# Layer 0's experts with the tokens stationary, loads ordered by first use, four PSUM banks for layer 1's first batch, and new orders for layer 0's turns

## Chip, core, metric

One core of one Trainium2 chip. The metric is the device time of one execution in microseconds; three runs of the kernel before gave 2697.05, 2699.24 and 2699.74 us, median 2699.24.

## What is computed

Four layers on an input `x` of 16 batches x 256 tokens x 128 features. Each layer normalises `x` and adds an attention (or state space) part and a feed-forward part:

```python
x  = L0_attn_x
xn = layernorm(x)
x  = x + L0_attn(xn) + L0_ffn(xn)   # 16-head attention, then a Mamba block; 32 experts
xn = layernorm(x)
x  = x + L1_attn(xn) + L1_ffn(xn)   # 16 heads of 64; feed-forward in FP4 blocks of 16
...                                 # layers 2 and 3: not touched by the change

# L0_ffn: every expert picks 8 tokens of each batch, and works on their weighted sum
merged = einsum('bked,bke->bed', tok, vals)        # [16 batches, 32 experts, 128]
h = gelu(einsum('bei,eih->beh', [merged, 1], w1))  # w1 [32, 129, 512]
o = einsum('bej,ejo->beo', [h, 1], w2)             # w2 [32, 513, 128]
out = scatter_add(o * vals)                        # back to the tokens picked
```

## The kernel before, in words

Five queues (TensorE `pe`, VectorE `ve`, ScalarE `ac`, GpSimd `po`, and `sp`, which issues nearly all DMAs) run lists of instructions that wait on each other's semaphores. A stage is a Python generator; its pieces are laid out between `yield`s, and `merge` interleaves the stages that run side by side by the places given in the table `ORDER` (lines 228 to 302), a list of numbers for each engine and stage. So the order of the work within a turn is written out by hand, per engine, and every turn of a layer has the same order.

**Load** (`load`, L2353). SP issues `x` (2 MB in rows of 512 bytes), then the packs `wf`, `wf0`, `wb` (masks and identity) and `wfc` (convolution weights). All engines wait for all packs, VectorE for `x` also. VectorE casts the masks to bf16 (L2363), TensorE multiplies two weights into `w_step` (L2367), ScalarE takes an exponential, VectorE builds `w_tap` (L2378). SP stores zeros twice. Then all five engines meet at a barrier (`phase_end`).

**Layer 0** (`layer0`, L2404). `pre` of a batch (L330, L1064, L1681) normalises it, turns it, computes the gate of the experts and `q`, `k`, `v`, all through one PSUM bank, so that its steps alternate between TensorE and the engine that empties the bank. For its idle filler `pe_idle` (L324) TensorE multiplies the mask by the identity with no use of the result. `pre` of batch 0 runs alone, `pre` of batch 1 beside the first row maxima (`FIRST[0]`). Then 19 turns follow. Turn t has `pre` of batch t+2, `wide` (scores, maxima, exponentials, values) of t, `out` and `inner` of t-1 (attention output; Mamba projections, `delta`), `states` of t-2 (eight pieces of the scan, each with two reads of 512 KB from DRAM that SP issues, a product and a scan on VectorE, a product on GpSimd and a sum over the states on TensorE, L868), and `results` of t-3. Turns 0 to 2 lack the later stages, turns 16 to 18 the earlier ones.

**Layer 0's experts** (`experts0`, L2430), after a barrier. For each of 32 experts: TensorE holds 128x128 blocks of `w1` stationary and moves 128 columns (16 tokens of 8 experts, of which one expert's 16 are used), 4 matmuls (L911); VectorE adds the bias (L1527); ScalarE applies GELU (L1990); TensorE does the same with `w2` (L924), 4 matmuls; VectorE adds the bias (L1532). All are fp32. Beside it VectorE quantises layer 1's feed-forward weights in three pieces (`ve_fp4` L1544, three operations per expert from expert 12 on) and TensorE turns them in nine (L973), VectorE copies them (L1604). Weights come in DMAs of 256 KB into 8 + 8 buffers; the first 8 experts are loaded behind the last reads of layer 0 (L2425), then `wf1` (3.2 MB), then the other 24.

**Layer 1** (`layer1`, L2449) begins after another barrier with `pe_spread1` of batches 0 and 1 and then `pre1` of batch 0 alone: 8 steps of two 256-column matmuls (L404), each emptied by ScalarE (L1719), and 4 steps of one 512-column matmul (L409), each emptied by VectorE (L1128), all through bank 4, each waiting until the bank has been read.

## Time and profile before

| | us |
|---|---|
| three runs, median | 2699.24 |
| profiled execution, its own time | 2694.34 |
| its span, first to last instruction | 2692.9 |
| load, to the barrier | 24.0 |
| layer 0 before its experts | 24.0 to 909.9 |
| layer 0's experts | 910.0 to 971.4 |
| layer 1 begins | 971.5 |

The page's busy shares of the span are TensorE 81%, VectorE 73%, ScalarE 53%, GpSimd 29%. A share is an average over stages with different limits, so the prediction reads stretches of the span instead. "PEclk" is the clock that TensorE was granted: 1.00 is 2.4 GHz, 0.50 is 1.2 GHz, and what lies between is a mix of the two over the stretch. One fp32 matmul of the program is two records in the trace (x8 is four matmuls).

### The profile page before, as it was taken

How to read it: one execution, taken by the hardware profiler on the slowest of the kernel's cores; microseconds unless marked ns; L12 is line 12 of the kernel's file. 1: busy time of each engine (PE TensorE's matmuls, PEld its weight loads, DVE VectorE, ACT ScalarE, POOL GpSimd, SP SyncE). 2: the span in 40 equal slices, each digit the busy share in tenths (PEclk: the TensorE clock that was granted, in tenths of full speed). 3: DMA queues.
4: the chain of work that ended last, by engine and by line, in shares of the span. 5: the costliest groups of instructions: out<-in, count | busy, mean ns of one | idle time of the engine just before them, and what ended most of it. 6: DMA issues, size and time to landing. Idle time of an engine off the chain costs nothing.

```text
span 2692.9 us, 47200 instructions
## 1 busy us (share of the span) xinstructions
PE 2176.3 (81%) x18050; PEld 1497.0 (56%) x18205; DVE 1959.5 (73%) x3999; ACT 1428.7 (53%) x3672; POOL 775.5 (29%) x460
## 2 busy tenths in 40 slices
PE   4678877887875678999999999868888986887886
PEld 2445555554542555666666666645565655555553
DVE  3389999899888537777777777745666642799997
ACT  1355565555554216767767676613343432566664
POOL 0034444443445302333323333310000000344443
PEclk9899899898987778999999999979999998778876
DMA  2077777786788940000000000000100000788886
GB/s 84 14 181 183 189 178 191 173 198 168 175 215 214 283 140 1 1 1 1 1 1 1 1 1 1 1 27 22 30 23 16 6 22 22 181 197 195 198 194 155
DMA packets 114320, 261.84 MB, mean 97 GB/s; under 512 B 13552, under 2 KB 55280, under 8 KB 113584
## 3 DMA queue, kind: packets, MB, share of 16 engines
q1 hardware_dynamic: 112048, 254.63, 37.6%
...
## 4 chain that ended last, share of the span: by engine, by line
PE 50%; DVE 20%; ACT 12%; DMA 8%; issue 8%; SPq 2%; another core or an unknown queue 0%; POOL 0%; POOLq 0%; DVEq 0%; ACTq 0%
DMA h<-dtu_rows 6%; PE psum L327 3%; DVE h L1481 3%; PE psum L695 3%; PE psum L691 3%; ACT pr L1840 3%; PE psum L582 3%; PE psum L743 3%; PE psum L404 2%; PE psum L627 2%; PE psum L702 2%; PE psum L431 2%; DVE mx L1396 2%; ACT pt L1884 2%; PE psum L700 2%
## 5 line engine op out<-in xcount | busy, mean ns | idle before, releaser
L2083 POOL TENSOR_TENSOR h<-h,Crep 128x1024 f32<-128x1024 f32 x128 | 322.4, 2520 | 563.9 <-DVE h L1481 563.9
L2067 POOL TENSOR_TENSOR pr<-pr,rsum 128x512 f32<-128x512 f32 x192 | 236.0, 1236 | 548.2 <-DVE rsum L1362 548.2
L1481 DVE TENSOR_TENSOR_SCAN h<-dA,h 128x1024 f32<-128x1024 f32 x128 | 305.2, 2387 | 18.8 <-ACT dA L1980 18.8
L1396 DVE TENSOR_REDUCE mx<-psum 128x4 f32<-128x1024 f32 (+1 forms) x192 | 230.2, 1216 | 106.0 <-PE psum L700 106.0
L1884 ACT ACTIVATE pt<-psum 128x1024 f32<-128x1024 f32 x192 | 189.1, 1020 | 142.1 <-PE psum L702 142.0
L1980 ACT ACTIVATE dA<-dA,A 128x255 f32<-128x255 f32 x512 | 215.6, 499 | 74.0 <-DMA dA<-delta_rows 73.6
L1840 ACT ACTIVATE pr<-psum,nb 128x256 f32<-128x256 f32 (+1 forms) x512 | 210.5, 429 | 15.9 <-DVE nb L1354 14.9
L2118 POOL TENSOR_TENSOR h<-h,Crep 128x1024 f32<-128x1024 f32 x64 | 151.3, 2364 | 223.2 <-DVE h L1289 223.2
L1850 ACT ACTIVATE prT<-psum 128x512 f32<-128x512 f32 x192 | 116.0, 604 | 149.7 <-PE psum L596 147.7
L1474 DVE TENSOR_TENSOR h<-h,psum 128x1024 f32<-128x1024 f32 x128 | 153.0, 1207 | 39.3 <-DMA h<-dtu_rows 39.1
L404 PE MATMUL psum<-xnT,pack_wf 128*128 128x256 f32 x512 | 148.4, 414 | 25.9 <-ACT qT L1719 18.6
L695 PE MATMUL psum<-qT,kT 32*128 32x256 f32 (+1 forms) x2048 | 123.2, 371 | 55.3 <-DVE mx L1396 54.8
L1350 DVE TENSOR_REDUCE mx<-psum 128x2 f32<-128x512 f32 (+1 forms) x192 | 130.5, 679 | 27.0 <-PE psum L586 16.4
L1289 DVE TENSOR_TENSOR_SCAN h<-dA,h 128x1024 f32<-128x1024 f32 x64 | 148.5, 2320 | 0.1
L327 PE MATMUL psum<-mask,identb 128*128 128x512 bf16 x433 | 123.5, 417 | 28.5 <-DVE qT L1089 20.0
...
L695 PEld LDWEIGHTS psum<-qT,kT 32*128 32x128 f32 x2048 | 86.9, 206 | 89.0 <-DVE mx L1396 69.9
L691 PE MATMUL psum<-kT,qT 32*128 32x128 f32 (+1 forms) x2048 | 115.4, 352 | 25.5 <-ACT pt L1884 13.2
L582 PE MATMUL psum<-kT,qT 64*128 64x256 f32 (+1 forms) x1024 | 112.4, 350 | 27.0 <-ACT pr L1840 27.0
L404 PEld LDWEIGHTS psum<-xnT,pack_wf 128*128 128x128 f32 x512 | 93.6, 198 | 63.6 <-ACT qT L1719 27.6
L743 PE MATMUL psum<-pt,v 128*32 128x256 f32 (+1 forms) x2048 | 96.5, 329 | 30.5 <-ACT pt L1884 29.9
L1792 ACT ACTIVATE dA<-dA,A 128x255 f32<-128x255 f32 x256 | 108.3, 495 | 21.8 <-DMA dA<-delta_rows 21.7
...
## 6 DMA issues: line engine op xcount, KB each, us to landing
dA<-delta_rows SPq DMA_DIRECT2D x192, 512.0 KB
h<-dtu_rows SPq DMA_DIRECT2D x192, 512.0 KB, 6.5
...
pack_wf<-wf SPq DMA_DIRECT2D x1, 3192.0 KB, 11.8
...
```

What stands on the lines that cost most here:

```text
L327: k.pe.e.matmul(bk[:, :], k.w["identb"], k.w["mask"], start=True, stop=True, skip_group_check=True)
L404: i = pe.e.matmul(B4[:, (g - g0) * L:(g - g0 + 1) * L], w[f"w{n}1"][:, g, :], xnT[:, :], start=True, stop=True)
L582: pe.e.matmul(k.bank[r][:, n * wid:(n + 1) * wid], qT[rows, g, q * P:(q + 1) * P], kT[rows, g, 0:wid], start=n == 0, stop=True, skip_group ...
L691: pe.e.matmul(banks[r][:, cols], qT[row:row + 32, g, q0:q0 + P], kT[row:row + 32, kg, 0:wid], start=n == 0, stop=True, skip_group_check=True)
L695: pe.e.matmul(banks[r][:, cols], kT[row:row + 32, kg, k0:k0 + P], qT[row:row + 32, g, k0:L], start=n == 0, stop=True, skip_group_check=True)
L1396: ve.e.tensor_reduce(mx[:, qb, 2 * h:2 * h + 2, groups[0]:groups[-1] + 1], k.psum[:, base:base + 2, :].rearrange("p i (n x) -> p i n x", n ...
L1481: ve.e.tensor_tensor_scan(flat(h), flat(k.dA[n % NDA]), flat(h), 0.0, ALU.mult, ALU.add).then_inc(*k.set("scanned", 0, n))
L1840: i = ac.e.activation(pr[:, h * wid:(h + 1) * wid], bk[:, h * wid:(h + 1) * wid], ACT.Exp, bias=nb[:, h:h + 1], scale=float(HD[1]) ** -0.5 ...
L1884: ac.e.activation(k.pt[2 * c + h][:, :], k.psum[:, base:base + 2, :].rearrange("p i x -> p (i x)"), ACT.Exp, scale=float(HD[l]) ** -0.5).t ...
L1980: i = ac.e.activation(dA[:, s, 1:], dA[:, s, 1:], ACT.Exp, scale=k.A0[:, n % 8, s:s + 1])
L2067: po.e.tensor_tensor(p3, p3, bcast(k.rsum[n][:, 0:len(heads[r])], P * (q + 1), 2), ALU.mult).then_inc(*k.set("normed", 1, b, p, r))
L2083: po.e.tensor_tensor(h[:, :, :], h[:, :, :], bcast(k.Crep[b % 2][:, :], 4, 1), ALU.mult).then_inc(*k.set("hC", 0, n))
```

## The change

1. **Load.** The first four tiles of `x`, `wf` and `wf0` go first and are all that TensorE, VectorE and ScalarE wait for. `pre` of batch 0 runs next. Casts, `w_step`, `A` and `w_tap` follow in `prepare_*`, behind it. The rest of `x` is loaded last. The barrier goes. The two filler matmuls of `pre` of batch 0 go.
2. **Turns.** `ORDER[0]` is replaced (small swaps), and turns 0, 1, 2, 15, 16, 17 and 18 have orders of their own.
3. **Experts.** Four experts a group. 32 columns of `merged` are stationary for each expert in a column tile of its own, and `w1` is moving, 512 columns. ScalarE copies the result, TensorE turns it with four transposes, VectorE adds the bias, ScalarE applies GELU; the output matmuls hold the tokens in column tiles and move `w2`; ScalarE copies, TensorE transposes, VectorE adds. Weights come as 16 DMAs of 1 MB (two experts, 8 KB a partition), ten buffers, seven of them loaded behind the last reads. A quantisation runs in one go at groups 2, 3 and 5; the turns at groups 4, 6 and 8.
4. **Layer 1's first batch** goes through banks 5, 7, 2, 4 in rotation.

```diff
+def places(layer, turn):
+    return ORDER.get(f"{layer}.{turn}", ORDER[layer])
...
 ORDER = {
     0: {
-        "pe_pre0": (2, 8, 9, 13, 20, 21, 26, 34),
+        "pe_pre0": (5, 10, 11, 14, 21, 23, 30, 34),
-        "ve_out": (7, 8, 10, 16, 18, 22),
+        "ve_out": (2, 4, 8, 10, 15, 22),
-        "ve_states": (2, 4, 19, 21, 23, 25, 31, 34, 36, 37, 41, 43, 44, 45, 49, 50, 52),
+        "ve_states": (1, 3, 20, 23, 24, 25, 31, 34, 36, 37, 42, 43, 44, 45, 49, 50, 52),
...
+    '0.0': {
+        "pe_pre0": (4, 5, 6, 8, 11, 13, 14, 15),
+        "pe_wide0": (0, 1, 2, 3, 7, 9, 10, 12, 16, 17),
...
-LOADS = {"x": 0, "wf": 1, "wb": 2, "wf0": 3, "wfc": 0, "wf0e": 0, "wf1": 1, "wf2": 2, "wf3": 3}
+LOADS = {"x0": 0, "wf": 1, "wb": 2, "wf0": 3, "wfc": 4, "x": 5, "wf0e": 0, "wf1": 1, "wf2": 2, "wf3": 3}
...
-    pe_idle(k, bk, 2)
+    if b:
+        pe_idle(k, bk, 2)
...
+FIRST_BANKS = (5, 7, 2, 4)
+def bank_of1(k, b, n):
+    return k.bank[4 if b else FIRST_BANKS[n % 4]]
+def taken1(k, b, n):
+    if b == 0:
+        if n < 4:
+            return k.at("xnT", 1, 0)
+        n -= 3
+    return evacuated(k, 1, b, n - 1) if 0 < n <= len(QK[1]) else k.at("v", 1, b, n - 9) if n else k.at("xnT", 1, b)
...
-QUANT_AT = (12, 17, 22)
-TURN_AT = (18, 19, 20, 23, 24, 25, 28, 29, 30)
+EG = P // 32
+NG0 = E0 // EG
+NPAIR, NEARLY = 10, 7
+QUANT_AT = (2, 3, 5)
+TURN_AT = ((), (), (), (), (0, 1, 2), (), (3, 4, 5), (), (6, 7, 8), (), ())
 def pe_experts0(k):
+    for g in range(NG0 + 3):
+        x = g - 2
+        if 0 <= x < NG0:
+            pe.wait_ge(*k.at("hg", x))
+            if x:
+                pe.wait_ge(*k.at("o0", x - 1))
             for j in range(J):
+                for c in range(EG):
+                    i = pe.e.matmul(k.bank[4][32 * c:32 * c + 32, 0:P], flat(k.hg[x % 2][:, j, c:c + 2, :]), expert_w2(k, EG * x + c, j),
+                                    start=j == 0, stop=j == J - 1, tile_position=(0, 32 * c), skip_group_check=True)
+        x = g - 3
+            pe.e.transpose(k.bank[5][:, 0:P], k.o0[x % 2][:, :], w["ident"]).then_inc(*k.set("o0_turned", x))
+        x = g - 1
+            z = k.z[x % 2][:, :].rearrange("t (p j) -> t p j", j=J)
             for j in range(J):
+                i = pe.e.transpose(k.bank[2 + x % 2][:, j * P:(j + 1) * P], z[:, :, j], w["ident"])
+        if g < NG0:
+            for c in range(EG):
+                i = pe.e.matmul(k.bank[g % 2][32 * c:32 * c + 32, :], flat(k.merged[:, ex:ex + 2, :]), expert_w1(k, ex),
+                                start=True, stop=True, tile_position=(0, 32 * c), skip_group_check=True)
+        for i in TURN_AT[g]:
+            pe_weight1(k, i)
...
 def ac_experts0(k):
+        if g < NG0:
+            ac.e.activation(k.z[g % 2][:, :], k.bank[g % 2][:, :], ACT.Copy).then_inc(*k.set("z", g))
+        if g in QUANT_AT:
+            ac_weights1(k, QUANT_AT.index(g))
+        x = g - 1
+            ac.e.activation(k.hg[x % 2][:, :, 0:EG, :], k.hz[x % 2][:, :, :, :], ACT.Gelu).then_inc(*k.set("hg", x))
+        x = g - 2
+            ac.e.activation(k.o0[x % 2][:, :], k.bank[4][:, 0:P], ACT.Copy).then_inc(*k.set("o0", x))
...
 def sp_experts0(k, some):
+    for n in some:
+        if n >= NPAIR:
+            sp.wait_ge(*k.at("output0", (n - NPAIR) // 2))
+        sp.e.dma_start(flat(k.pairs[n % NPAIR]), k.ins["m_w"][n, :, :]).then_inc(*k.set(f"pair{n % NPAIR}", n, by=16))
...
 def load(k, packs):
+    sp.e.dma_start(k.X[:, 0:2 * QT, :], x[:, 0:2 * QT, :]).then_inc(*k.set(*landed("x0"), by=16))
+    for pname in ("wf", "wf0", "wb", "wfc"):
+        sp_load(k, pname, packs[pname])
+    sp.e.dma_start(k.X[:, 2 * QT:, :], x[:, 2 * QT:, :]).then_inc(*k.set(*landed("x"), by=16))
...
+    for q in (pe, ve, ac):
+        for pname in ("x0", "wf", "wf0"):
+            q.wait_ge(*k.at(*landed(pname)))
...
+def prepare_ve(k):
+    ve.wait_ge(*k.at(*landed("wb")))
+    for n, t in k.small:
+        ve.e.tensor_copy(t[:, :], w[n])
+    ve.wait_ge(*k.at("dt", "weights"))
+    ve.e.tensor_copy(flat(k.w_step), k.bank[0][:, :])
+    ve.wait_ge(*k.at("A_exp", 0))
+    ve.e.tensor_scalar(k.A[:, :, :], k.A[:, :, :], -1.0, None, ALU.mult)
+    ve.wait_ge(*k.at(*landed("wfc")))
+    for j in range(CONV):
+        i = ve.e.tensor_tensor(k.w_tap[:, j, :, :], w["w_in"][:, 0:CI, :], w["conv_rows"][:, j, :, :], ALU.mult)
+    i.then_inc(*k.set("prepared"))
+    ve.wait_ge(*k.at(*landed("x")))
...
 def layer0(k, t0e):
         run(pre(k, 0))
+        prepare(k)
         merge(FIRST[0], (first(k, 0), e + "_first"), (pre(k, 1), e + "_pre0"))
...
-    sp_experts0(k, range(8))
+    sp_experts0(k, range(NEARLY))
```

## Rows read from the trace of the kernel before

**Rows 1.** The page's head.
```profile
span 2692.9 us, 47200 instructions
```

**Rows 2.** Stretches: us, busy us of each engine (instructions), clock, DMA share, GB/s.
```profile
0.00:24.00 24.00, 2.04 (x4) 1.16 (x4) 4.25 (x20) 1.51 (x2) 1.16 (x5) 1.00 0.70 235
...
64.00:108.00 44.00, 29.78 (x278) 18.43 (x280) 16.01 (x32) 10.33 (x20) 0.00 (x0) 0.79 0.01 1
108.00:155.00 47.00, 33.75 (x317) 22.83 (x319) 23.20 (x43) 20.88 (x41) 2.35 (x1) 0.95 0.41 101
...
248.00:840.00 592.00, 463.37 (x4369) 304.26 (x4412) 535.40 (x623) 340.00 (x690) 243.72 (x99) 0.91 0.77 188
840.00:880.00 40.00, 19.33 (x121) 10.32 (x120) 33.95 (x24) 19.11 (x44) 20.83 (x8) 0.67 0.90 222
880.00:910.00 30.00, 9.82 (x68) 3.55 (x66) 21.64 (x14) 5.33 (x14) 17.80 (x6) 0.59 0.84 228
...
910.00:972.00 62.00, 60.28 (x522) 58.83 (x522) 31.83 (x120) 11.13 (x37) 0.45 (x1) 1.00 0.80 257
...
976.00:1013.00 37.00, 25.68 (x46) 12.00 (x45) 3.83 (x10) 7.49 (x19) 0.00 (x0) 0.51 0.25 95
```

**Rows 3.** Timeline of batch 0's `pre`: start us, us, engine, line, [idle before].
```profile
24.01 0.49 DVE L1040 BATCH_NORM_STATS2 stats<-X 128x6 f32<-128x128 f32 x2 [2.26 <-SPq L179]
...
35.02 1.04 PE L327 MATMUL psum<-mask,identb 128*128 128x512 bf16 x2 [0.97 <-DVE qT L1089]
...
40.40 0.16 DVE L1104 TENSOR_TENSOR v<-psum,pack_wf 128x16 f32<-128x16 f32 x1
```

**Rows 4.** DMA issues (KB each, us to landing), and stretches of the load.
```profile
pack_wf<-wf SPq DMA_DIRECT2D x1, 3192.0 KB, 11.8
...
pack_wf<-wf SPq DMA_DIRECT2D x1, 1326.5 KB, 7.3
...
6.00:8.00 2.00, 0.00 (x0) 0.00 (x0) 0.00 (x0) 0.00 (x0) 0.00 (x0) 1.00 1.05 288
...
14.00:16.00 2.00, 0.00 (x0) 0.00 (x0) 0.00 (x0) 0.00 (x0) 0.00 (x0) 1.00 1.00 406
```

**Rows 5.** The chain of waits near the end of layer 0: start us, us, what.
```profile
880.77 12.06 DMA h<-dtu_rows
```

**Rows 6.** Page and timeline: what the experts' new steps are costed by.
```profile
L1850 ACT ACTIVATE prT<-psum 128x512 f32<-128x512 f32 x192 | 116.0, 604 | 149.7 <-PE psum L596 147.7
...
380.60 1.17 PE L691 MATMUL psum<-kT,qT 32*128 32x128 f32 x32
...
383.53 1.07 PE L868 MATMUL psum<-h,pack_wf 128*32 128x256 f32 x16
...
862.50 0.64 PE L868 MATMUL psum<-h,pack_wf 128*32 128x256 f32 x8 [1.30 <-POOL h L2083]
...
914.63 1.06 PE L911 MATMUL psum<-merged,w1r 128*128 128x128 f32 x8
...
932.78 0.54 DVE L1550 TENSOR_REDUCE f4s<-pack_wf 128x24 f32<-128x384 f32 x1
...
940.14 0.56 DVE L1588 SCALAR_TENSOR_TENSOR wgu_q<-pack_wf,f 128x384 uint32<-128x384 uint32 x1
```

**Rows 7.** Timeline: layer 1's first batch, and TensorE's clock coming back.
```profile
906.00 1.91 PE L327 MATMUL psum<-mask,identb 128*128 128x512 bf16 x4 [0.33 <-issue]
...
908.58 0.61 PE L890 MATMUL psum<-pack_wf,yT 128*128 128x128 f32 x4
...
978.65 2.07 PE L404 MATMUL psum<-xnT,pack_wf 128*128 128x256 f32 x4 [1.53 <-ACT xnT L1711]
980.76 0.84 ACT L1719 ACTIVATE qT<-psum,pack_wf 128x256 f32<-128x256 f32 x2 [2.16 <-PE psum L404]
...
1011.26 2.08 PE L409 MATMUL psum<-pack_wf,xnT 128*128 128x512 f32 x2 [0.78 <-DVE v L1128]
...
1024.49 1.03 PE L404 MATMUL psum<-xnT,pack_wf 128*128 128x256 f32 x4
```

More of the change, by code:

```diff
@@ L401, in pe_pre1 @@
         yield
[L402 removed]
+        pe.wait_ge(*taken1(k, b, j))
         for g in range(g0, g0 + 2):
[L404 removed]
+            i = pe.e.matmul(bank_of1(k, b, j)[:, (g - g0) * L:(g - g0 + 1) * L], w[f"w{n}1"][:, g, :], xnT[:, :], start=True, stop=True)
         i.then_inc(*k.set("qk", 1, b, j))
@@ L407, in pe_pre1 @@
         yield
-        pe.wait_ge(*(k.at("v", 1, b, j - 1) if j else evacuated(k, 1, b, 7)))
-        pe.e.matmul(B4[:, 0:cn], xnT[:, q * P:(q + 1) * P], w["wv1"][:, c0:c0 + cn], start=True, stop=True).then_inc(*k.set("v_mm", 1, b, j))
+        pe.wait_ge(*taken1(k, b, len(QK[1]) + j))
+        pe.e.matmul(bank_of1(k, b, len(QK[1]) + j)[:, 0:cn], xnT[:, q * P:(q + 1) * P], w["wv1"][:, c0:c0 + cn], start=True, stop=True).then_inc(*k.set("v_mm", 1, b, j))
 def pe_pre2(k, b):
@@ L930, in pe_ffn, with expert_w1, expert_w2 @@
+def expert_w1(k, ex):
+    return k.pairs[ex // 2 % NPAIR][:, ex % 2, 0:H0]
+def expert_w2(k, ex, j):
+    return k.pairs[ex // 2 % NPAIR][:, ex % 2, H0 + j * D:H0 + (j + 1) * D]
 def pe_ffn(k, b):
@@ L2387, in load, with prepare_ac, prepare_pe @@
     sp.wait_ge(*k.at("delta_stored1", "zero"))
-    for q in (k.pe, ve, ac, k.po, sp):
-        phase_end(k, q, "load")
+    ac.e.preload_act_table_set("natural_log_exp_and_others")
+    for x in k.x1T:
+        ve.e.memset(x[:, 0:CONV - 1], 0.0)
+    for v in k.v:
+        ve.e.memset(v[:, :, :, 9:], 0.0)
+        ve.e.memset(v[:, :, :, 8:9], 1.0)
+    for q in (pe, ve, ac):
+        for pname in ("x0", "wf", "wf0"):
+            q.wait_ge(*k.at(*landed(pname)))
+def prepare_ac(k):
+    ac = k.ac
+    ac.e.activation(k.A[:, :, :], k.w["A_log0"], ACT.Exp).then_inc(*k.set("A_exp", 0))
+    ac.wait_ge(*k.at("prepared"))
+def prepare_pe(k):
+    pe, w = k.pe, k.w
+    for m in range(CI):
+        i = pe.e.matmul(k.bank[0][:, m * DI:(m + 1) * DI], w["w_dtin"][:, m * P:(m + 1) * P], w["w_dt"], start=True, stop=True)
+    i.then_inc(*k.set("dt", "weights"))
+    pe.wait_ge(*k.at("prepared"))
+def prepare_ve(k):
+    ve, w = k.ve, k.w
+    ve.wait_ge(*k.at(*landed("wb")))
+    for n, t in k.small:
+        ve.e.tensor_copy(t[:, :], w[n])
+        w[n] = t[:, :]
+    ve.wait_ge(*k.at("dt", "weights"))
[7 more added lines that the diff above has]
+    ve.wait_ge(*k.at(*landed("x")))
 def turn0(k, t, e, pre, out, wide, inner, states, results, summing=None):
-    merge(ORDER[0],
+    merge(places(0, t),
           (results(k, t - 3), e + "_results") if results is not None and 0 <= t - 3 < NB else None,
@@ L2405, in layer0 @@
     k.slot_read, k.pre_read = [None] * 4, None
-    for e, pre, first in (("pe", pe_pre0, pe_first_max), ("ve", ve_pre0, ve_first_max)):
+    for e, pre, first, prepare in (("ve", ve_pre0, ve_first_max, prepare_ve), ("pe", pe_pre0, pe_first_max, prepare_pe)):
         run(pre(k, 0))
+        prepare(k)
         merge(FIRST[0], (first(k, 0), e + "_first"), (pre(k, 1), e + "_pre0"))
     run(ac_pre0(k, 0))
+    prepare_ac(k)
     run(ac_pre0(k, 1))
@@ L2571, in build @@
     t0e = k.pack("wf0e")
-    k.w1r = [k.sb("w1r", [P, H0]) for i in range(8)]
-    k.w2r = [k.sb("w2r", [P, H0 // P, D]) for i in range(8)]
-    k.hz, k.hg = k.two("hz", [P, H0 // P, NB]), k.two("hg", [P, H0 // P + P // NB - 1, NB])
+    k.pairs = [k.sb("pair", [P, 2, 2 * H0]) for i in range(5)]
+    assert k.top <= k.onT_end
+    k.top = end0
+    k.pairs += [k.sb("pair", [P, 2, 2 * H0]) for i in range(NEARLY - 5)]
     layer0(k, t0e)
@@ L2579, in build @@
     place_ffn(k)
+    top, k.top = k.top, k.onT_end
+    k.z, k.o0 = k.two("z", [P, H0]), k.two("o0", [P, P])
+    k.hz, k.hg = k.two("hz", [P, H0 // P, EG, NB]), k.two("hg", [P, H0 // P, EG + 1, NB])
+    k.pairs += [k.sb("pair", [P, 2, 2 * H0]) for i in range(NPAIR - NEARLY)]
+    assert k.top <= k.ffn_at
+    k.top = top
     experts0(k, t1)
@@ L2666, in _packs @@
     w1, w2 = g["L0_ffn_w1"], g["L0_ffn_w2"]
-    put("m_b1", w1[:, D, :].reshape(E0, H0 // P, P).transpose(2, 0, 1))
+    put("m_b1", w1[:, D, :].reshape(E0, P, H0 // P).transpose(1, 2, 0))
     put("m_b2", w2[:, H0, :].T)
```

370 lines of the change are left out of this document (251 added, 119 removed).

## The prediction

> **What bounds the kernel now.** The page's shares name no engine for the whole span [rows 1], so I read the stretches that the change touches [rows 2]. The load, 24 us, has no engine busy above 4.25 us; it waits for DMAs and ends in a barrier. Between 64 and 108 us TensorE is busy 29.8 of 44 us at a clock of 0.79, and VectorE 16.0: nobody is full, steps wait for one another. In 248 to 840 VectorE is busy 535.4 of 592 us, 90%. From 840 to 910 the DMA share is 0.90 and 0.84, so the reads of the scan set the pace. The experts, 910 to 972, are pure TensorE: 60.3 of 62 us, at full clock. And 976 to 1013 is TensorE again, but by turns with the engine that empties its one bank, 25.7 of 37 us busy and at 0.51 of the clock.
>
> **The load.** Before, VectorE starts batch 0 at 24.01 [rows 3]. Afterwards it needs 0.26 MB of `x` in rows of 512 bytes, 0.15 and 1.36 MB of weights in long rows. The DMAs ran at 288 GB/s while `x` was coming and at 406 over the wide packs [rows 4]: 0.9 + 0.4 + 3.3 = 4.6 us, behind some 2.5 us until the first bytes move, and about 1 us to notice; 8.2 us in all. (`wf0` alone took 7.3 us from issue to landing [rows 4].) So batch 0 begins 15.8 us earlier. Its two fillers, 1.04 us at half clock, go [rows 3]; TensorE waited for nothing else there, so 1.0 us is saved. What was prepared behind the load, 4.25 us of VectorE less 0.3 of memsets, that now lie in front [rows 2], comes back after `pre` of batch 0, where TensorE waits for it: +4.0, plus 0.2 for the handover. ScalarE's exponential and TensorE's four matmul records run beside VectorE's casts. `wb`, `wfc` and the rest of `x`, 3.1 MB, land by some 17 us and are first wanted at 24 to 29. Sum -12.6 us, between -10 (landing at 10.8) and -14.
>
> **Layer 0's first turns.** Nothing is removed; steps change places. In the order of before, the second row maximum waits behind three steps of `pre`, and the exponentials behind that; in turn 0 of the new one the scores and maxima go first. What can be won is idle time of TensorE that no other full engine forces: 14.2 us in 64 to 108 and 13.3 in 108 to 155 [rows 2]. The trace doesn't show the new order. The bounds are a loss of 4 us (a step put ahead of its input blocks its queue) and a gain of 20 (three quarters of that idle time). I take a third, -9.
>
> **The steady turns.** The new common order moves about six of VectorE's 52 places and four of TensorE's, each by one or two steps. VectorE has 56.6 us of idle time in the twelve turns of rows 2. I take -2 us, with bounds of -12 (a fifth of the idle time) and +6, half a microsecond a turn.
>
> **The last turns.** These wait for DMA. The last read of the scan took 12.06 us to land [rows 5], with 4.2 MB of experts' weights issued right behind it; now there are 7.3 MB behind it, in longer rows, which could take more of the engines' turns. Against that the new orders bring `inner` of the last batches, and so their reads, earlier. 10 to 16% of 70 us of DMA is unused [rows 2]. I take -2, from -8 to +4. The early weights are all in by the barrier: about 1 MB of reads at 250 GB/s and 7.3 MB at 406 from 881 on end at about 903.
>
> **The experts.** Before: 256 matmuls of 128 columns, in 64 fours; four take 1.06 us [rows 6] and overlap, so that the 64 need about 57 us, 0.89 each, of a stage of 61.4. After, for a group of four experts at full clock: hidden, four matmuls of 512 columns side by side in four column tiles. Four of 256 columns took 0.64 us alone and 0.535 in a row (x16 in 1.07) [rows 6], so about 0.64 + 0.43 = 1.07. Transposes of z, 0.89. Output, 16 matmuls of 128 columns, four at a time: sixteen such, tiled by rows, took 1.17 [rows 6]. Transpose of o, 0.22. Together 3.35 us against 7.1 before, 27 for eight groups against 57. The trace has no stationary load with a stride, as z's has; I take it as the plain one, and up to double (+0.8 a group, of which half counts) for the bound.
>
> TensorE is then no longer the bound. Between hidden of one group and output of the group before stand, on ScalarE in this order, the copy of z (0.60 by rows 6), GELU (256 columns, 0.4 by rows 7) and the copy of o (estimated at 0.25 from the same row). And VectorE now does each quantisation in one go: before it ran from 932.78 to 940.70 with three experts' biases between, 1.1 us, so 6.9 us by itself [rows 6]; behind it wait bias, GELU, and output. The walk, from the start of the stage: ScalarE's table load 1.3; `wf1` lands at 11.8, as before [rows 4]; quantisation 0 to 18.9; bias of group 2 and output bias, 0.7; quantisation 1 to 26.6; three turns through the one bank, 0.3 for the transpose and 0.3 for the copy and the handovers, 2.5, to 29; output, transposes 2.4 and bias 0.5, to 32; quantisation 2 (a little smaller, 6.7) to 38.7; bias and turns to 41.3; then the rest of group 7, 3.5 + 2.9 with the last turns 2.5, output 7, copy, transpose, bias, to 53. The DMA has 12.7 MB to bring, 31 us at 406 GB/s, under that cover; pairs 10 to 15 wait for outputs 0, 1 and 2, which come by 20 us.
>
> 53 us holds at full clock. TensorE is busy 27 + 3 of 53, 57%, in pieces. In 840 to 880, with 48%, the clock was 0.67, and in 64 to 108, with 68%, 0.79 [rows 2]. I take 0.75; of TensorE's work some 11 us is on the walk, so +3: 56 us against 61.4, or -5.5. Bounds: `wf1` landing at 9.5 and a full clock -11; all at half clock and slow strided loads +1. By rows a tiled set costs 0.1 us more alone than in a row. The Trainium skill, "TensorEngine Tiling (Array Packing)", section "Tiling Modes", says that changing the tiling mode drains TensorE, and this kernel changes it four times a group. By this rule each change would show; at the 0.1 us of the rows that is 3 us over 32 changes, half of them off the walk, and the trace agrees as far as it goes.
>
> **Layer 1's first batch.** Before: eight steps of 3.0 us (2.07 on TensorE at half clock, 0.84 on ScalarE, handovers) and four of 2.86 (2.08, and 0.78 of waiting for VectorE) [rows 7], 34.6 us from 978.65. With four banks TensorE doesn't wait. It would need 12 x 2.07 = 24.9 us if its clock stayed at half: -9.7. But unbroken work brought the clock back: filler matmuls from 906.0 on ran at half rate, and at 908.58 four records took 0.61 us, full rate [rows 7]. So two steps at 2.07, then six at 1.07 and four at 1.03 (the same instruction at 1024.49 took 1.03 [rows 7]); ScalarE needs 0.89 a step and VectorE under 0.78, both less. 4.1 + 6.4 + 4.1 = 14.6: -20. The Trainium skill, "TensorE: Matmul & The Clock Gate", section "What's actually happening", says that half rate is the default and that activity lifts it. The trace agrees with it in both directions here. On the other side the handful of small steps before (973 to 978) now begins behind a less busy TensorE and may run at half rate: +1. Sum -19, between -21 and -9.
>
> **Sum.** -12.6 - 9 - 2 - 2 - 5.5 - 19 = -50 us on the profiled execution's 2694.3 (span 2692.9 [rows 1]), so 2644. The median of the runs is 4.9 us above it; the forecast for the median is 2699.2 - 50 = 2649.
>
> **Rivals.** (a) *Clock.* The sparse experts stage lets TensorE fall to half rate, and it stays there: experts -1, layer 1's first batch -10. Sum -37, 2662. For it: 0.51 at 69% busy in 976 to 1013 [rows 2]. Against it: 906 to 908.6. By the skill's rule above it would come out only if TensorE paused between the steps. Chance 0.15. (b) *The orders bring more.* VectorE's idle share in the steady turns falls by a fifth and the first turns gain 15: -66, 2633. For it is the idle time, against it that the swaps are small. 0.2. (c) *The first load isn't earlier*, because the first packs share the engines with all that is issued behind them and land near 16: -43, 2656. 0.08. (d) *Slower.* The common order makes VectorE wait in each of the 12 or 13 steady turns: `out` now stands ahead of `pre` and, with it, of the whole queue; if the turned heads aren't there, products and scans are late, and the DMA slots with them. It decides from 50 / 13 = 3.8 us a turn. At 4.7 us a turn it would be 2710. VectorE's idle share of 10%, 4.7 us a turn, speaks for little cover; that the batch's heads have been turned from the turn before speaks against. 0.04. The forecast, with the bounds of its terms, has the other 0.53.
>
> **Numbers.** The likeliest case gives 2649. Its own terms spread by about 10 us; the range down to (b) and up to (a) is 2630 to 2667. About 0.2%, 5 us, can be told from no change. Faster 0.94, same 0.02, slower 0.04.
>
> **What would show it.** Right: batch 0's first VectorE row near 8 us and the first scores near 28; the experts' stage 53 to 58 us long with TensorE under 65% busy and VectorE's quantisations unbroken; in layer 1's first batch L404's successor without ScalarE's waits and at about 1.03 us from the third step; steady turns of 48 to 49 us. Wrong: the stage of the experts above 62 or under 48 us; twelve steps of 2.07; steady turns that differ by over 1 us.

## The result, and the profile after

The changed kernel took 2611.2 us (median of 4 runs, 2610.98 to 2612.55), the kernel before beside it 2698.9: a ratio of 0.9674, 95% interval 0.9661 to 0.9686, or 87.7 us less. The forecast was 2649, with a range down to 2630. The direction was right, the size was not: 50 us were expected and 88 came.

The profiled execution has a span of 2609.3 us against 2692.9 [rows 1], 83.6 less, so the account below is made of these two. First the page's head, then stretches of the kernel after (columns as in rows 2; 236 to 695 are the ten steady turns, 861 to 914 the experts, 921 to 936 layer 1's first batch):

```profile
span 2609.3 us, 46686 instructions
```

```profile
236.00:695.00 459.00, 370.69 (x3725) 247.97 (x3767) 430.94 (x542) 282.53 (x576) 190.17 (x81) 0.97 0.82 194
861.00:914.00 53.00, 30.90 (x369) 16.57 (x369) 26.87 (x74) 11.69 (x28) 0.00 (x0) 0.84 0.59 243
921.00:936.00 15.00, 14.06 (x52) 10.25 (x54) 3.39 (x7) 7.47 (x19) 0.00 (x0) 0.78 0.51 195
```

Then its timeline (start us, us, engine, line, [idle before <-releaser]) at batch 0's first row, the first scores, layer 0's last addition to `X`, the last expert's bias, and layer 1's first batch:

```profile
9.90 0.48 DVE L1248 BATCH_NORM_STATS2 stats<-X 128x6 f32<-128x128 f32 x2 [8.75 <-DMA pack_wf<-wf]
...
29.09 2.09 PE L873 MATMUL psum<-kT,qT 32*128 32x256 f32 x16 [2.21 <-DVE w_tap L2629]
...
860.94 0.42 DVE L1720 TENSOR_TENSOR X<-X,psum 128x256 f32<-128x256 f32 x1 [1.81 <-PE psum L1074]
...
913.94 0.27 DVE L1743 TENSOR_TENSOR oall<-psum,pack_wf0e 128x64 f32<-128x64 f32 x1 [0.48 <-PE psum L1106]
...
921.94 9.93 PE L586 MATMUL psum<-xnT,pack_wf 128*128 128x256 f32 x32 [1.53 <-ACT xnT L1922]
931.71 3.60 PE L591 MATMUL psum<-pack_wf,xnT 128*128 128x512 f32 x8
935.23 1.16 PE L764 MATMUL psum<-kT,qT 64*128 64x128 f32 x16
```

The steady turns are read most safely from one instruction that comes once a turn, the addition that makes `x1T`. One line of the code in a window from batch 3 to batch 13 gives eleven of them, with the first and the last start; so ten turns. The same row of the kernel before and after (line, engine, operation, count: shortest/median/longest in ns, first and last start us):

```profile
L1441 DVE SCALAR_TENSOR_TENSOR x1T<-psum,pack_wf,xnT x11: 466/466/476, 256.5 to 746.0; 128x256 f32<-128x256 f32 x11
```

```profile
L1649 DVE SCALAR_TENSOR_TENSOR x1T<-psum,pack_wf,xnT x11: 452/454/484, 236.0 to 694.8; 128x256 f32<-128x256 f32 x11
```

To the hundredth the starts are 256.53 and 745.98 before, 235.95 and 694.82 after: ten turns took 489.4 us and take 458.9, **48.9 us a turn before, 45.9 after**. Put together by stages:

| stage | forecast | measured |
| --- | --- | --- |
| to the first scores (40.6 to 29.1) | -12.6 | -11.5 |
| on to `x1T` of batch 3 | -9 | -9.1 |
| ten steady turns (batch 3 to 13) | -2 (for twelve) | -30.6 |
| rest of layer 0 | -2 | +2.7 |
| end of layer 0 to layer 1's first such matmul | -5.5 | -8.2 |
| layer 1's first batch (34.6 to 13.3) | -19 (with +1 of the row above) | -21.3 |
| everything behind it | 0 | -5.6 |

Of the last row, 2.0 us lie between the end of layer 1's first batch and the first gather of layer 3 (1257.4 us before, 1255.4 after), and 3.6 in the stretch from layer 3's first to its last gather (336.1 and 332.5). Layer 3's code is the same. That stretch took between 332.5 and 336.3 us in the profiles of this study, whether a kernel had this change or not, and the changed kernel profiled once more (e15) took 336.2 there; so these 3.6 us are spread between executions.

So one term failed, the steady turns.

### The profile page after: what moved, and what is told of

The parts are those of the page before. It is cut to its first block, busy times and chain, and to the rows that moved or that the text cites. A ratio compares the mean times of both kernels' runs of the same rounds, so it can differ in the third digit from the quotient of the medians.

```text
span 2609.3 us, 46686 instructions
## 1 busy us (share of the span) xinstructions
PE 2125.4 (81%) x17896; PEld 1447.2 (55%) x18051; DVE 1927.3 (74%) x3952; ACT 1427.9 (55%) x3664; POOL 771.3 (30%) x460
## 4 chain that ended last, share of the span: by engine, by line
PE 45%; DVE 21%; ACT 12%; DMA 8%; issue 7%; SPq 2%; another core or an unknown queue 0%; POOL 0%; POOLq 0%; DVEq 0%; ACTq 0%
DMA h<-dtu_rows 7%; DVE h L1689 4%; PE psum L492 3%; PE psum L877 3%; ACT pr L2052 3%; PE psum L764 3%; PE psum L873 3%; PE psum L925 2%; PE psum L809 2%; PE psum L586 2%; PE psum L613 2%; PE psum L884 2%; DVE mx L1558 2%; PE psum L748 1%; PE psum L882 1%
## 5 line engine op out<-in xcount | busy, mean ns | idle before, releaser
L1689 DVE TENSOR_TENSOR_SCAN h<-dA,h 128x1024 f32<-128x1024 f32 x128 | 297.2, 2327 | 5.8 <-ACT dA L2192 5.8
L586 PE MATMUL psum<-xnT,pack_wf 128*128 128x256 f32 x512 | 141.6, 402 | 19.9 <-ACT qT L1930 14.9
L877 PE MATMUL psum<-qT,kT 32*128 32x256 f32 (+1 forms) x2048 | 116.0, 353 | 39.9 <-DVE mx L1604 39.4
L1497 DVE TENSOR_TENSOR_SCAN h<-dA,h 128x1024 f32<-128x1024 f32 x64 | 148.3, 2318 | 0.1
L492 PE MATMUL psum<-mask,identb 128*128 128x512 bf16 x432 | 114.6, 394 | 18.9 <-ACT qT L1903 7.4
L586 PEld LDWEIGHTS psum<-xnT,pack_wf 128*128 128x128 f32 x512 | 92.1, 194 | 52.8 <-ACT qT L1930 20.9
```

Of the source, the lines that this page charges most:

```text
L492: k.pe.e.matmul(bk[:, :], k.w["identb"], k.w["mask"], start=True, stop=True, skip_group_check=True)
L586: i = pe.e.matmul(bank_of1(k, b, j)[:, (g - g0) * L:(g - g0 + 1) * L], w[f"w{n}1"][:, g, :], xnT[:, :], start=True, stop=True)
L877: pe.e.matmul(banks[r][:, cols], kT[row:row + 32, kg, k0:k0 + P], qT[row:row + 32, g, k0:L], start=n == 0, stop=True, skip_group_check=True)
L1689: ve.e.tensor_tensor_scan(flat(h), flat(k.dA[n % NDA]), flat(h), 0.0, ALU.mult, ALU.add).then_inc(*k.set("scanned", 0, n))
```

## Experiments

### Is it the common order? (e1, e2)

e1 is the kernel before with one thing changed, the dictionary `ORDER[0]`; e2 is the changed kernel with the old `ORDER[0]`:

```diff
 # e1, in the kernel before (e2: the reverse, in the kernel after)
 ORDER = {
     0: {
-        "pe_inner": (11, 18, 19, 23, 32),
+        "pe_inner": (9, 19, 20, 24, 27),
...
```

> The kernel before with the new common order of layer 0's turns in the place of the old one, for all turns; nothing else of the change. Theory A (the common order alone makes the steady turns shorter): the ten turns from x1T of batch 3 to that of batch 13 take 459 us (45.9 a turn) in place of 489.4, and the whole about 2665 (2655 to 2672). Rival B (the steady turns are shorter because the special first turns leave the batches in another phase, or because of the earlier load): 489 us for those ten turns, and 2695 to 2702 in all. Rival C (both are needed): in between, some 475 us and 2684.

> The changed kernel with the old common order in the turns that have no order of their own (3 to 14); load, special turns, experts and banks as changed. Theory A: the ten steady turns are back at 489 us, and the whole is 2611 + 30 to 38 = 2641 to 2649. Rival B: the ten turns stay at 459 and the time at 2611 to 2614. Rival C: some 475 us, 2627.

e1: 2660.0 us against 2700.0 on its chip, ratio 0.9854 (0.9823 to 0.9885), `x1T` from 256.2 to 709.9, 45.4 us a turn. e2: 2652.3 us (up to 2649 expected), 239.0 to 731.6, 49.3 a turn. Theory A holds on both sides: the common order alone makes the turn shorter, with the old load and with the new one. The profiles with the whole old order in these turns give 48.9 to 49.4 us a turn and those with the whole new one 45.4 to 45.9, so a difference of a few tenths says nothing.

### Which engine's list? (e5, e6, e7, e9)

Each is the kernel before with the new lists of some engines only (e5: `pe_*`, e6: `ve_*`, e7: `ac_*`, e9: all but `ve_*`, so SyncE's too).

> The kernel before with the new common order of layer 0's turns for TensorE alone; VectorE's, ScalarE's and SyncE's as before. The steady turns (ten, from x1T of batch 3 to that of batch 13) were 48.9 to 49.4 us with the old common order and 45.4 to 45.9 with the new one in five profiles. Theory A1 (TensorE's swaps carry the gain: the fourth inner step ahead of the fifth wide one, and sum1 ahead of pre4): 46 us a turn. Theory A2 (VectorE's order carries it: out ahead of pre, the third inner step ahead of states' ninth): 49. Theory A3 (the lists only gain together, since a step that moves on one engine waits for its partner on another): 49 or longer.

> The same for VectorE alone. A1: 49 us a turn. A2: 46. A3: 49 or longer, as VectorE then waits for turned heads that TensorE gives later.

> The same for ScalarE alone (out ahead of the first wide step, the third inner step ahead of states' third). A1 and A2: 49 us a turn. A3: 49 or longer. A fourth theory, A4 (ScalarE's order carries it: the products of inner reach VectorE earlier): 46.

> The kernel before with the new common order for TensorE, ScalarE and SyncE, VectorE's as before. After e5 to e7 (TensorE's alone 50.8 us a turn, ScalarE's 51.1, VectorE's 49.0, all of them 45.4) theory A3 holds, that the lists gain only together. Theory A3a (TensorE and ScalarE are the pair, in out and inner, and VectorE adds little): 45.5 to 46.5 us a turn. Theory A3b (all three are needed, since VectorE's place of out or inner blocks both): 48 to 52.

Per turn: TensorE's alone 50.8, VectorE's alone 49.0, ScalarE's alone 51.1, TensorE's and ScalarE's together 46.8. Single runs took 2730.6, 2697.0, 2740.5 and 2671.2 us, beside medians of the kernel before of 2700.4 (the first three) and 2694.2. Two of the three lists make the kernel slower by 30 and 40 us when they come alone. The waits in ten turns show why (who waited <- for whom: us in total, times, longest us), first e5, then e7:

```profile
DVE merged L1098 <- PE psum L367: 44.3, 10, 5.3
...
PE psum L367 <- ACT Crep L1968: 37.5, 10, 4.7
```

```profile
ACT Crep L1968 <- PE psum L840: 51.0, 10, 5.3
```

`pre` and the fifth inner step share one PSUM bank, and each use waits for the reader of the one before. The new TensorE list puts the matmul of `Crep` earlier. If ScalarE's list doesn't bring its copy forward too, the next step of `pre` stands in TensorE's queue for 3.75 us a turn, and VectorE behind it for 4.4; if only ScalarE's moves, the copy blocks ScalarE for 5.1. These two moves must come together. That much of theory A3 is right.

### Which part of the turn? (e10 to e14)

e10 has the new order up to the fourth wide step and the old one behind it, e11 the reverse. e13 and e14 divide the moves of e11; here the lists of e13 that differ from before, then the steps that e14 moves:

```diff
-        "pe_inner": (11, 18, 19, 23, 32),
+        "pe_inner": (11, 18, 19, 23, 26),
-        "pe_pre0": (2, 8, 9, 13, 20, 21, 26, 34),
+        "pe_pre0": (2, 8, 9, 13, 20, 21, 30, 34),
-        "ac_inner": (14, 15, 17, 19, 25),
+        "ac_inner": (14, 15, 17, 19, 23),
...
```

```diff
 # e14, as sequences of steps (numbered from the one ahead of the first yield)
-PE   ... pre4 pre5 summing2 inner3 summing3 ...
+PE   ... pre4 summing2 pre5 inner3 summing3 ...
-ACT  ... inner2 states4 inner3 wide3 ... states7 inner4 wide5 ...
+ACT  ... inner2 inner3 states4 wide3 ... wide5 states7 inner4 ...
-DVE  ... inner2 states10 inner3 ... states13 pre13 wide5 wide6 ...
+DVE  ... inner2 inner3 states10 ... states13 wide5 wide6 pre13 ...
```

> The kernel before with the new order in the first part of a steady turn on all three engines (up to TensorE's and VectorE's fourth wide step and ScalarE's third of states: out ahead of summing, pre and wide), the old order behind it. Theory H (the first part carries the gain, as the heads' output leaves its bank earlier): 46 us a turn. Theory T (the second part carries it: fourth inner step ahead of the fifth wide one, third inner step ahead of states): 49. Both needed: 47 to 49, and the sum of the two gains 3.5.

> The complement of e10: the old order in the first part of a steady turn, the new one behind it. Theory H: 49 us a turn. Theory T: 46. If the gains add up, the two runs' gains against 48.9 to 49.4 sum to about 3.5.

> The kernel before with one pair of moves in the common order: on TensorE the fifth inner step (the matmul of Crep, in pre's bank) ahead of the sixth wide one and the step of pre with the merged sums behind the seventh; on ScalarE the fifth inner step (the copy of Crep) ahead of the seventh of states. In e5, TensorE's list alone, that step of pre waited 3.75 us a turn for the copy of Crep; in e7, ScalarE's alone, the copy waited 5.1 us a turn for the matmul. Theory P (this pair, moved on both engines, is the gain of e11; the once-a-turn wait of 3.6 us of a score step for a row maximum goes with it): 46.3 to 47 us a turn. Theory Q (the rest of the second part carries it): 49.

> The complement of e13: the second part's other moves (TensorE's third step of summing ahead of pre's sixth, ScalarE's fourth inner step ahead of states' fifth, VectorE's fourth inner step ahead of states' eleventh), the pair left as before. Theory P: 48.5 to 49.5 us a turn. Theory Q: 46.3 to 47. Together the two gains should come to the 2.6 to 3 us of e11.

Per turn: e10 48.7, e11 46.3, e13 49.1, e14 46.1 (2701.0, 2662.4, 2705.1 and 2665.0 us in single runs). The kernel before had medians of 2694.2 beside the first two and 2691.0 beside the others. The second part carries nearly all of it, and within it not the pair that my theory P had named: e13 is as slow as before, and e14 has 2.8 us of the 3.1. Theory P fell.

### The cause: two instructions that can't run side by side (e17, e18)

What the faster kernels have in common, and the kernel before, e10 and e13 lack, is one short row. VectorE's clamp of `zab` (`min` with 1e19, 128 x 512 float32) by its line, in the kernel before and after, ten turns each:

```profile
L1454 DVE TENSOR_SCALAR zab<-zab x10: 1547/2562/2570, 271.1 to 713.7; 128x512 f32<-128x512 f32 x10
```

```profile
L1662 DVE TENSOR_SCALAR zab<-zab x10: 387/398/402, 252.2 to 666.9; 128x512 f32<-128x512 f32 x10
```

The same instruction, on a tile of the same shape, took 2.56 us and takes 0.40. Timeline of one turn of the kernel before:

```profile
513.66 2.28 DVE L1481 TENSOR_TENSOR_SCAN h<-dA,h 128x1024 f32<-128x1024 f32 x1
...
515.21 0.84 ACT L1959 ACTIVATE zab<-psum,pack_wf 128x256 f32<-128x256 f32 x2 [2.95 <-PE psum L834]
...
516.02 2.35 POOL L2083 TENSOR_TENSOR h<-h,Crep 128x1024 f32<-128x1024 f32 x1 [4.76 <-DVE h L1481]
516.09 2.56 DVE L1454 TENSOR_SCALAR zab<-zab 128x512 f32<-128x512 f32 x1
518.57 1.21 DVE L1396 TENSOR_REDUCE mx<-psum 128x4 f32<-128x1024 f32 x1
...
522.68 0.66 DVE L1467 TENSOR_TENSOR dtu<-delta,su 128x512 f32<-128x512 f32 x1
```

And of the kernel after:

```profile
481.39 2.27 DVE L1689 TENSOR_TENSOR_SCAN h<-dA,h 128x1024 f32<-128x1024 f32 x1
483.59 0.39 DVE L1662 TENSOR_SCALAR zab<-zab 128x512 f32<-128x512 f32 x1
483.74 2.46 POOL L2310 TENSOR_TENSOR h<-h,Crep 128x1024 f32<-128x1024 f32 x1 [3.23 <-DVE h L1689]
483.91 1.21 DVE L1604 TENSOR_REDUCE mx<-psum 128x4 f32<-128x1024 f32 x1
```

VectorE's scan releases both GpSimd's product and, being the instruction ahead, VectorE's clamp. Before, the clamp also waited for ScalarE's exponential, which came 0.1 us too late: GpSimd started at 516.02, the clamp at 516.09, and it ended at 518.65, 0.28 behind the product (518.37). After, the exponential is there when the scan ends, the clamp starts at once, and GpSimd starts 0.15 us later. The row maximum behind the clamp, for which TensorE's next score step waits, moves by the same 2.2 us. Only certain instructions shut each other out: that same row maximum ran beside GpSimd's product in the kernel after, and took the 1.21 us that it took before, when the product had ended.

TensorE brings it about. In the turn of before it does `pre`'s sixth step (L327, with a wait for VectorE's `qT`) ahead of the third step of summing (L868), and `dt` (L834) behind both:

```profile
511.63 0.38 PE L327 MATMUL psum<-mask,identb 128*128 128x512 bf16 x1 [1.20 <-DVE qT L1089]
...
512.18 1.07 PE L868 MATMUL psum<-h,pack_wf 128*32 128x256 f32 x16
513.18 1.99 PE L834 MATMUL psum<-su,w_step 128*128 128x256 f32 x8
```

Summing waits for nothing there; put ahead, it fills the wait, and `dt` comes earlier. That is one swap of two places, e17:

```profile
498.52 1.07 PE L868 MATMUL psum<-h,pack_wf 128*32 128x256 f32 x16
499.79 0.38 PE L327 MATMUL psum<-mask,identb 128*128 128x512 bf16 x1 [0.20 <-issue]
...
500.82 1.99 PE L834 MATMUL psum<-su,w_step 128*128 128x256 f32 x8 [0.41 <-DVE gvT L1095]
```

From the end of TensorE's step before these to `dt` it is 2.75 us in the turn of before and 2.23 in e17.

e18 keeps the collision and changes how much of it VectorE sees. The edits of both:

```diff
 # e17
-        "pe_pre0": (2, 8, 9, 13, 20, 21, 26, 34),
+        "pe_pre0": (2, 8, 9, 13, 20, 22, 26, 34),
-        "pe_summing": (5, 6, 22, 24, 31),
+        "pe_summing": (5, 6, 21, 24, 31),
 # e18
-        "ve_inner": (1, 38, 40, 42),
+        "ve_inner": (1, 39, 40, 42),
-        "ve_wide0": (9, 11, 13, 29, 39, 47, 48),
+        "ve_wide0": (9, 11, 13, 29, 38, 47, 48),
```

> The kernel before with one swap in one list: TensorE does its third step of summing (16 matmuls that wait for nothing there) ahead of pre's sixth step (which waited 1.2 us for qT each turn), so that the matmuls of dt, ScalarE's exponential and VectorE's clamp of zab come about 1 us earlier, and the clamp is ready when the scan before it ends. Theory G (VectorE's clamp and GpSimd's product of the scan can't run side by side, and who starts second waits out the other: the old order lets GpSimd win by 0.07 us): the clamp takes 0.39 us in place of 2.56, a steady turn 46 to 47 us, and the whole 25 to 35 us less than before. Rival (the clamp's length is a sign and not the cause, or ScalarE's and VectorE's moves are needed for it): the clamp stays at 2.5 us or the turn at 48.5 us or more.

> The kernel before with one swap in another list: VectorE takes the row maximum that TensorE waits for ahead of the clamp of zab, so that the clamp starts some 1.2 us into GpSimd's product and not at its start. Theory G: the clamp still ends about 0.3 us behind GpSimd's product, so it takes 1.2 to 1.5 us in place of 2.56, the 3.6 us wait of a score step for a row maximum is down to 1 or 2, and a turn takes 47.3 to 48.3 us. Rival (the clamp is slow for another reason, such as its place behind a scan): it takes 0.39, or 2.56 again.

e17, the clamp and `x1T`, then e18:

```profile
L1454 DVE TENSOR_SCALAR zab<-zab x10: 389/402/405, 268.7 to 694.7; 128x512 f32<-128x512 f32 x10
L1441 DVE SCALAR_TENSOR_TENSOR x1T<-psum,pack_wf,xnT x11: 465/466/484, 253.1 to 724.7; 128x256 f32<-128x256 f32 x11
```

```profile
L1454 DVE TENSOR_SCALAR zab<-zab x10: 1679/1684/1690, 268.5 to 712.9; 128x512 f32<-128x512 f32 x10
...
512.53 2.36 POOL L2083 TENSOR_TENSOR h<-h,Crep 128x1024 f32<-128x1024 f32 x1 [4.69 <-DVE h L1481]
513.48 1.69 DVE L1454 TENSOR_SCALAR zab<-zab 128x512 f32<-128x512 f32 x1
...
515.87 0.48 DVE L1460 SCALAR_TENSOR_TENSOR delta<-psum,pack_wf,zab 128x256 f32<-128x256 f32 x1 [0.70 <-ACT zab L1963]
```

e17, one swap on TensorE: the clamp is at 0.40 in every turn, 47.2 us a turn, ratio 0.9937 (0.9919 to 0.9954), 17 us by the ratio. The mechanism is as expected, the gain is smaller than the 25 to 35 I wrote: 1.8 us a turn of the 3.1. The swap also fills TensorE's wait, and that could be a gain of its own. The rows speak for the clamp: VectorE's busy time falls from 44.9 to 43.0 us a turn and its idle time stays (4.0 and 4.1), while a gain that came through TensorE would show as less waiting on VectorE. That is an argument from the rows and not a test. e14 is e17 with moves on ScalarE and VectorE beside it, and has 46.1 a turn; all lists have 45.4 to 45.9. What e14 adds is idle time of VectorE, 4.1 down to 2.9 us a turn: in ten turns its waits for the reads of `h` fell from 21.8 to 14.5 us and those for the matmul of `qT` from 10.3 to 1.5. Which of its moves does which was not tried.

e18: the clamp starts 0.95 us into GpSimd's product and ends 0.28 us behind it (515.17 against 514.89), in each of the ten turns: not 0.40 and not 2.56, but what is left of the product and 0.3. The turn, though, stayed at 49.1 (ratio 1.000, 0.9989 to 1.0012), where I expected 47.3 to 48.3: the row maximum came earlier (TensorE's longest wait for it fell from 3.8 to 1.2 us), but `delta` now waited 0.7 us a turn for ScalarE's logarithm, behind the later clamp, and VectorE's waits for the reads of `h` rose from 13.2 to 28.4 us in ten turns. So a shorter clamp is worth nothing where VectorE then waits for something else; why those reads come later I have not shown.

The count over all kernels agrees: where TensorE's third summing step stands ahead of `pre`'s sixth (the changed kernel and what was built on it, e1, e5, e9, e11, e14, e17) the median clamp takes 0.39 to 0.40 us, and in the others (before, e2, e3, e6, e7, e10, e13, e18) 1.7 to 2.6. One steady turn of e8, a version of the changed kernel described below, has the collision by itself: the exponential came late, GpSimd led by 0.8 us, the clamp took 1.82, and the turn 49.1 us, where the other nine took 44.7 to 46.4. e5 shows that the fast clamp alone doesn't win: it had 0.39, and lost more at the bank of `Crep` (VectorE idle 7.7 us a turn).

The Trainium skill, "SBUF — State Buffer", section "Who interferes with whom", says that VectorE and GpSimd share a port pair under an exclusive lock: whichever starts first holds it for the whole instruction, and the other blocks; it names `tensor_scalar` among the operations that can take it. The traces agree: 0.07 us of lead for GpSimd costs VectorE 2.2 us, and 0.95 us of lead costs it 1.3.

### Four banks (e3)

```diff
 # e3: bank_of1() and taken1() of the change in the kernel before, nothing else
-        pe.wait_ge(*(evacuated(k, 1, b, j - 1) if j else k.at("xnT", 1, b)))
+        pe.wait_ge(*taken1(k, b, j))
...
```

> The kernel before with four banks for layer 1's first batch, and nothing else of the change. If its worth doesn't hang on the experts' stage before it: from the first of the batch's matmuls to the end of the last 13 to 14 us in place of 34.6, and 2699 - 21 = 2678. Rival: behind the busier old experts' stage the first steps run at full rate too, 12 to 13 us, -22. Rival: the time is given back in the rest of layer 1 (its first feed-forward waits for weights or for VectorE), then 2685 to 2695.

2676.2 us against 2700.0, ratio 0.9911 (0.9877 to 0.9946). From the first matmul to the next stage:

```profile
984.38 9.29 PE L420 MATMUL psum<-xnT,pack_wf 128*128 128x256 f32 x32 [1.53 <-ACT xnT L1727]
993.50 3.60 PE L425 MATMUL psum<-pack_wf,xnT 128*128 128x512 f32 x8
997.03 1.16 PE L598 MATMUL psum<-kT,qT 64*128 64x128 f32 x16
```

The batch takes 12.65 us in place of 34.6 [rows 7], which is the rival's 12 to 13 and not the 13 to 14 that I had put first. In the changed kernel it was 13.3 (921.94 to 935.23), 0.6 more; it comes there behind the sparser experts. Nothing is given back in layer 1: from the end of the batch to layer 3's first gather e3 took 1255.6 us and the kernel before 1257.4.

### The special turns (e12)

```diff
 def places(layer, turn):
-    return ORDER.get(f"{layer}.{turn}", ORDER[layer])
+    return ORDER[layer]
```

> The changed kernel without orders of their own for turns 0, 1, 2 and 15 to 18, the new common order in all of them. In e1 the stretch from x1T of batch 0 to that of batch 3 took 137.7 us with the common order alone, in the changed kernel 138.9, and the last turns 75.1 against 72.0. Theory (the special orders are worth little in the first turns and about 3 us in the last): 138 and 75 us here, 2611 + 1 to 5 in all. Rival (turn 0's own order is what brings x1T of batch 0 forward by the last 2 or 3 us): x1T of batch 0 at 100 or later, 2617.

2620.6 us, ratio 0.9737 (0.9713 to 0.9760), some 6 us more by the ratios than the changed kernel in e15 (2614.9 us, ratio 0.9715, 0.9689 to 0.9741); the intervals overlap, so the whole times alone don't decide. `x1T` of batch 0 came at 103.9; in the profiles with the own order of turn 0 it came between 96.9 and 100.2. That is the rival, and it holds: up to there turn 0's order is worth 4 to 7 us. The others I can't tell from spread: batch 0 to 3 took 137.8 us here and 134.6 to 138.9 with the special orders, batch 13 to the end of layer 0 165.1 here and 164.4 to 168.2 with them.

### A better experts' stage (e4, e8, e16 against e15)

The forecast had VectorE's unbroken quantisations on the stage's path. e4 issues them in pieces and turns ScalarE's order. e8 is e4 with three weights turned into one bank and one or two copies behind, and with ScalarE's absolute values, which the quantisation needs, ahead of its copy of `z`:

```diff
 # e4
-QUANT_AT = (2, 3, 5)
+QUANT_AT = (3, 5, 7)
+PIECES = 6
...
-        for _ in quant:
-            pass
+        for _ in range(PIECES + (g in QUANT_AT)):
+            next(quant, None)
...
 # e8, in pe_weight1 and ve_weight1
+    for n in range(3):
+        rows = min(P, I1 - n * P)
+        if i < 2:
+            x = pe.e.transpose(B6[:, n * P:n * P + rows], k.wgu_q[0:rows, 3 * i + n, :], w["ident"][0:rows, 0:rows])
...
+        x = ve.e.tensor_copy((k.wgT, k.wuT)[i][:, :], B6[:, 0:I1])
```

> The changed kernel with two things new in layer 0's experts: the three quantisations are issued in pieces of six steps per group over groups 3 to 8 instead of in one go each, with the turning of their weights a group later, and ScalarE does GELU of the group before ahead of the copy of z. Theory (the stage's path is VectorE's three unbroken quantisations, with TensorE idle behind them, and ScalarE's order): from the last X add of layer 0 to the last output bias 44 to 46 us in place of 53, and 2602 to 2604 in all. Rival (the path is TensorE with its handovers, or the DMAs of the pairs): 52 to 53 us and 2610 to 2612. Rival (the denser stage also lifts TensorE's clock at layer 1's first batch): 2 us more.

> The kernel of e4 with the turning of layer 1's quantised weights three at a time into one bank, with one or two copies behind (in place of three transposes and three copies by turns), and ScalarE's absolute values ahead of the copy of z. In e4 the stage stayed at 52.8 us: what the pieces gave was taken by the turning, in which TensorE waited 3.0 us for VectorE's copy behind six pieces, twice, and ScalarE 6.2 to 6.8 for the bias behind it, twice, and by 3.5 us of VectorE's wait for ScalarE's absolute values. If that is so: the stage takes 44 to 47 us. Rival (what is left is TensorE at half rate with its handovers): 50 to 52.

> The changed kernel itself, on the chip of e16: 2605 to 2615 us, and 45.5 to 46 us a steady turn; the stage of the experts 53 us. The last layer's scan took 332.5 us in its first profile and 332.5 to 336 in the profiles of kernels that leave it alone, so 333 to 336 here if that is nothing but spread.

> The kernel of e8 once more, beside the changed kernel: the stage of the experts 44 to 45 us, and 8 to 9 us less than e15 in the medians. If its gain is lost in a busier chip or another clock in layer 1, 0 to 4 us less.

e4: 2608.6 us, ratio 0.9662 (0.9630 to 0.9693), not to be told from the changed kernel's 0.9674. Its stage took 52.8 us, where I had expected 44 to 46. The wait had only moved: TensorE turns a weight, and then stands behind VectorE's copy, which stands behind six pieces:

```profile
887.84 0.33 PE L1190 MATMUL psum<-pack_wf,wgu_q 128*128 128x128 f32 x1 [2.97 <-DVE wgT L1824]
```

In e8 TensorE turns three weights before it waits. It ran in 2599.9 us, ratio 0.9641 (0.9609 to 0.9673). Its stage, and then that of the changed kernel in e15:

```profile
852.80:897.00 44.20, 31.21 (x369) 16.21 (x369) 26.06 (x69) 12.06 (x28) 0.00 (x0) 0.92 0.71 290
```

```profile
864.70:919.80 55.10, 34.51 (x369) 18.41 (x369) 27.11 (x74) 11.69 (x28) 0.00 (x0) 0.78 0.57 232
```

44.2 us against 55.1 (53.3 in the first profile); e16, the same kernel again, took 44.2 too. TensorE's granted clock was 0.92 and 0.96 in the two profiles of the new stage, 0.84 and 0.78 in those of the changed kernel. Its same 369 matmuls took 31.2 and 29.9 us against 30.9 and 34.5, so it was busy for anything between 0.3 us more and 4.6 less. Most of the 9 to 11 us is TensorE's idle time, 22.4 and 20.6 us in the changed kernel, 13.0 and 14.3 here. The pieces alone gave nothing, and what the turning alone would give was not tried. On one chip, with the same runs of before: the changed kernel 2614.9 us, ratio 0.9715 (0.9689 to 0.9741), e16 2601.0, ratio 0.9671 (0.9642 to 0.9699). **The version of e16 beats both kernels**, the changed one by 14 us in the medians, and its slowest run (2608.3) is under the other's fastest (2612.3); I expected 8 to 9.

## Why the forecast was right and wrong

**The load** (-12.6, measured -11.5 at the first scores). VectorE began at 9.90, not at 8.2: the first weights landed 1.7 us later than the transfers at the rates of rows 4 make. In the profiles of the other kernels with this load it began at 8.7 to 10.2. Behind it the terms held. Rival (c) is out.

**The first turns** (-9, measured -9.1). That the number is right is luck in part: "a third" of TensorE's idle time named no wait. From the first scores to `x1T` of batch 0 it took 71.5 us and takes 68.0. The common order alone lost there (77.9 in e1, 75.2 in e12), and turn 0's own order won it back and 3.5 us more. The other 5.5 us are between batches 0 and 3 (144.4 and 138.9), where the common order alone gives 137.7 (e1). There collisions end too: in the kernel before the clamps of batches 1 and 2 took 2.56 us each, in e1 0.39 and 0.40. In the changed kernel that of batch 2 took 0.39, but that of batch 1, whose turn has an order of its own, still 2.03.

**The steady turns** (-2 for twelve, measured -30.6 for ten). This is the step that failed: "I take -2 us, with bounds of -12 (a fifth of the idle time) and +6". The bound took VectorE's 90% busy as work that no order can change, so only idle time could be won. Per turn VectorE's busy time fell from 45.0 to 43.1 us, its idle time by 1.2. The 1.9 us of busy time were the clamp (22.7 us in its ten records before, 4.0 after), recorded as busy while it waited inside for GpSimd. The 1.2 us of idle time came with the moves on ScalarE and VectorE, as e14 beside e17 has it (1.3); in ten turns they fill the whole of the bound of -12 by themselves. That the swaps are small, the argument for -2, told nothing: one swap of neighbours is worth 1.8 us a turn, while the one that moves furthest, VectorE's fourth of `out` (from place 16 to 10, and not "one or two" steps), lies in the first part, which gave nearly nothing (e10). The same stretch of the kernel before as a row:

```profile
256.00:746.00 490.00, 388.90 (x3721) 256.25 (x3760) 449.69 (x544) 281.40 (x573) 198.16 (x81) 0.92 0.75 183
```

The row was there to be read: 2.56 us for 128 x 512 elements with one input, beside 0.66 for a `tensor_tensor` of the same shape (L1467, above), and 1.5 to 2.6 in one line. Rival (b), "the orders bring more", had the right sign at -66 and the wrong mechanism, a fifth of the idle share.

**The last turns** (-2, measured +2.7 from batch 13 on, -2.1 from batch 15 on). Within the bounds. From batch 15 on the profiles of this study took 71.9 to 76.0 us with either order (74.1 before, 72.0 after, 74.7 in e12), so no gain of the orders there can be told from spread.

**The experts** (-5.5, measured -8.2 with the start of layer 1). The walk gave 53 us at full clock and 56 with the half rate's share; the last bias ended at 914.21, 53.3 behind 860.94, and 55.1 in e15. The clock was 0.84 there and 0.78 in e15; I had taken 0.75. TensorE was 58% busy, as said. Of the path only a part is shown: pieces in place of VectorE's unbroken quantisations changed nothing until the turning of the weights went too (e4, e8). A group's rows on TensorE were shorter than the 3.35 us of the walk. Behind one another at full clock they took 2.8 (881.56 to 884.37):

```profile
881.56 1.08 PE L1098 MATMUL psum<-pair,hg 128*32 128x128 f32 x32 [2.16 <-ACT o L2219]
882.57 0.33 PE L1106 MATMUL psum<-pack_wf,o 128*128 128x128 f32 x1
882.74 0.65 PE L1114 MATMUL psum<-pack_wf,z 128*128 128x128 f32 x4
883.31 1.06 PE L1123 MATMUL psum<-pair,merged 128*32 128x512 f32 x8
```

They also show two changes of the tiling (128*32 to 128*128 and back) and not the four of the prediction, and no gap at either; a price of 0.1 us for each, as the forecast allowed, is not to be seen.

**Layer 1's first batch** (-19, measured -21.3). The first matmuls were at half rate for three steps of about 1.7 to 2.1 us and not for two, then 1.0 and below, as ScalarE's starts show (924.05, 925.75, 927.46, 928.45, 929.32, with eight activations in the next 3.43). Rival (a), the clock that stays at half, is out. So is (d), a slower common order, for the whole; e5 and e7 show how near it was: with one engine's list wrong it costs 1.9 to 2.2 us a turn.
